# A graph layer whose second half is moved into the turns of its gathers

## The reference

```python
xn = layernorm(x)
def gnn_layer(x, row, col, W, b, g, beta):
    agg = segment_sum(x[col], row)              # one gathered row per edge
    deg = maximum(segment_sum(1, row), 1)
    h = (x + agg / deg) @ W.T + b
    return silu(layernorm(h) * g + beta)
x = x + gnn_layer(gnn_layer(xn)) + mix(xn)      # mix: per-node QKV, small blocks, w_res, hyperbolic scalings
y = layernorm(x)
w = softmax(((y @ W_x + b_x) @ W_slice + b_slice) / temp)   # 8 heads x 64 slices per node
token = normalised sum over nodes of w * (y @ W_fx + b_fx)
out_slice = attention(token)                    # 8 small 64x64 attentions
x = x + (sum over slices of w * out_slice) @ W_out + b_out
```

## Time and profile before

| | |
|---|---|
| median of 3 runs | 2936.33 us (2932.64 to 2941.06) |
| profiled execution | 2949.13 us, span 2947.2 us |
| busy: PE, ACT, DVE, POOL | 75%, 55%, 48%, 56% of the span |
| mean granted TensorE clock | 0.873 |
| first gather of layer 0 | 298.3 us |
| last gather of layer 1 | 2423.3 us |

### The profile page before, as it was taken

The page is one execution under the profiler, slowest core; times in us unless marked ns, Lnnn a source line. Parts: engine busy times, 40 slices in busy tenths (PEclk is TensorE's granted clock), DMA queues, the critical chain, the costliest instruction groups (busy, mean ns, idle before and its releaser), DMA issues.

```text
span 2947.2 us, 34117 instructions
## 1 busy us (share of the span) xinstructions
PE 2224.6 (75%) x8923; PEld 1618.1 (55%) x8923; DVE 1404.6 (48%) x3188; ACT 1624.0 (55%) x3910; POOL 1645.6 (56%) x1745
## 2 busy tenths in 40 slices
PE   0776677777778787669487778778787658899999
PEld 0542456565656665555355656566565545455577
DVE  8899513443434443327523434344343215899611
ACT  7410465666666666536556666666666533565422
POOL 0000777777777777740477777777777771344300
PEclk9887688998888898878788989888898876899999
DMA  7200333333333333351333333333333347200002
GB/s 181 70 18 0 98 109 109 114 109 112 113 113 110 114 111 108 111 145 46 114 109 109 113 112 111 111 113 114 111 110 110 109 113 174 72 18 9 1 18 70
DMA packets 101271, 280.80 MB, mean 95 GB/s; under 512 B 29211, under 2 KB 43369, under 8 KB 97088
## 3 DMA queue, kind: packets, MB, share of 16 engines
q0 software_dynamic: 75904, 210.74, 25.1%
q1 hardware_dynamic: 12184, 55.08, 7.0%
q10 hardware_dynamic: 13000, 12.80, 1.5%
HBM read 252.91 MB, written 25.60 MB: 95 GB/s over the span
## 4 chain that ended last, share of the span: by engine, by line
POOL 50%; PE 17%; issue 17%; DVE 14%; DMA 1%; ACT 1%; DVEq 0%; ACTq 0%; SPq 0%; POOLq 0%
POOL big L566 50%; PE ps L1161 3%; PE ps L1262 3%; DVE arena_a L1296 3%; DVE arena_a L1297 3%; PE ps L1128 2%; PE ps L1150 2%; PE ps L1042 1%; PE ps L1144 1%; PE ps L1254 1%; PE ps L1159 1%; DVE big L1733 1%; DMA big<-table,arena_a 1%; DVE big L1734 1%; DVE lnst L1340 1%
## 5 line engine op out<-in xcount | busy, mean ns | idle before, releaser
L566 POOL DMA_INDIRECT big<-table,arena_a x1568 | 1509.6, 963 | 709.1 <-issue 476.7
L1042 PE MATMUL ps<-big 128*125 x3968 | 1073.5, 431 | 504.0 <-SPq L461 308.0
L1042 PEld LDWEIGHTS ps<-big 128*125 128x125 f32 x3968 | 833.3, 214 | 716.7 <-issue 565.4
L1629 DVE TENSOR_TENSOR big<-ps,big 125x257 f32 x496 | 211.0, 425 | 1263.5 <-PE ps L1042 1240.4
L697 ACT ACTIVATE arena_b<-iota_row,arena_a 128x125 f32<-128x125 f32 x1984 | 601.3, 386 | 62.2 <-PE ps L1042 28.2
L699 ACT ACTIVATE big<-arena_b,ones 128x1000 f32<-128x1000 f32 x248 | 280.0, 1129 | 8.1
L720 ACT ACTIVATE nodes<-nodes 125x512 f32<-125x512 f32 x50 | 31.6, 632 | 305.1 <-DVE nodes L1687 305.1
L1683 DVE RECIPROCAL nodes<-nodes 125x512 f32<-125x512 f32 x50 | 167.7, 3353 | 1.7
L1061 PE MATMUL ps<-arena_b,nodes 128*125 128x384 f32 x400 | 165.4, 538 | 0.0
L594 POOL TENSOR_TENSOR arena_b<-arena_b,head 125x512 f32<-125x512 f32 x50 | 55.0, 1100 | 161.9 <-DVE head L1741 161.9
L555 POOL IOTA big<- 1x992 f32 x1 | 0.9, 948 | 195.0 <-DVEq L1419 195.0
(11 more groups left out here) (387 smaller groups left out, 3159.7 us busy)
## 6 DMA issues: line engine op xcount, KB each, us to landing
big<-table,arena_a POOLq DMA_INDIRECT x1568
table<-nodes SPq DMA_DIRECT2D x9, 1120.0 KB
nodes<-table SPq DMA_DIRECT2D x4, 1680.0 KB
nodes<-table ACTq DMA_DIRECT2D x50, 125.0 KB
mix_rows<-nodes ACTq DMA_DIRECT2D x50, 125.0 KB
nodes<-in_x_dram SPq DMA_DIRECT2D x5, 1120.0 KB
big<-mix_rows SPq DMA_DIRECT2D x5, 1120.0 KB
nodes<-in_x_dram SPq DMA_DIRECT2D x10, 560.0 KB
```

The source lines that it names most:

```text
L566: pool.indirect_dma_start(gat[:, GRP * slot + k, 0:D], None, table[l], bass.IndirectOffsetOnAxis(ap=s_dst[:, n:n + 1], axis=0)).then_inc(s ...
L1042: mm = pe.matmul(ps[0:PT, SUM_BANKS[q % SB], 0:257], onehot[:, ROUND * (r % 2) + QS * k + n, :], gat[:, bass.ds(slots[QS * k + n], 1), :]. ...
L1629: dve.tensor_tensor(at, ps[0:PT, SUM_BANKS[q % SB], 0:257].unsqueeze(1), at, ALU.add).then_inc(s("agg_added"), 1)
```

## The change

- Tiles are ranked by their number of edges at the start: ScalarE counts for tiles 1 to 33, VectorE for the others; 50 rounds of "equal to t, times rank" on VectorE, added up by TensorE, give each edge its tile's rank, and the sort (levels 1 to 7 now behind this) goes by rank. `acc` of layer 1 is in order of rank; `order_row` turns a rank back into a tile number for transfers.
- Tile k's quads are complete by quad 5(k + 1).
- All 50 mix tiles stand in layer 0's window, one slot behind every half round (2 quads).
- In layer 1's window a planner (`second_layer_plan`) lists for 272 ticks, 248 of them with a quad, which of 16 stages of which tiles stand behind the quad on each engine: U (u), T (transpose), H (product), B (statistics), S and R (root and reciprocal for a group of tiles), Z (norm and Tanh), X (x2), V and Q (its root and reciprocal), C (normalised row), D (transpose), L (logits), M (maximum, subtraction, Exp), N (sum, reciprocal, product), W (sum over nodes). Quads of layer 1 use 2 banks instead of 4.
- The folds of the slice weights stand behind quads 0 to 3 of layer 1 (`set_up`).
- ScalarE starts the loads of x1, x and mix rows a few tiles ahead and stores x2 tile by tile; GpSimd does nothing in layer 1 but gather; the products that GpSimd made go to VectorE. x2 is read back at the end, and each output tile is stored by itself.

```diff
-SUM_BANKS = (3, 4, 5, 7)
+SUM_BANKS = ((3, 4, 5, 7), (6, 7))
+QUADS_A_TILE = 5
-NM = NT // 2
-EARLY = (0, 3)
+NM = NT
+HALVES = 2 * NSL // ROUND
+AHEAD = 2
...
+GROUPS = [6, 6, 6, 6, 6, 6, 5, 4, 2, 1, 1, 1]
+STAGES = ("W", "N", "M", "L", "D", "C", "Q", "V", "X", "Z", "R", "S", "B", "H", "T", "U")
+PE_COST = {"W": 1.9, "L": 1.0, "D": 0.35, "H": 1.4, "T": 0.35}
+DVE_COST = {"N": 1.6, "M": 1.5, "X": 1.8, "Z": 1.1, "S": 1.5, "V": 1.5, "B": 0.45, "U": 0.6}
...
+                if any(at.get(one, tick) >= tick for one in need):
+                    break
+                if st == "U" and tick < min(QUADS_A_TILE * (k + 1), NQ) - 1:
+                    break
+                if items and (pe + PE_COST.get(st, 0) > 2.3 or dve + DVE_COST.get(st, 0) > 3.1):
+                    break
...
+def window(step, slot):
+    for half in range(max(HALVES, SLOTS)):
+        if half < HALVES:
+            step(half)
+        if half < SLOTS:
+            slot(half)
...
-            for t in range(1, NT + 1):
+            for t in range(1, SUMMED):
                 ins = act.activation(counted, bin_f, ACT.Relu, bias=bin_id[0:PT, t:t + 1], scale=-1.0, accum_out=counts[0:PT, t:t + 1])
...
+            for t in range(NT):
+                pe.wait_ge(s("eq_made"), t + 1)
+                for k in range(2):
+                    mm = pe.matmul(ps[0:PT, k, 0:EQ // 2], ident_b[:, :], eq_ring[t % EQ_RING][:, k * EQ // 2:(k + 1) * EQ // 2], start=(t == 0), stop=(t == NT - 1))
+                mm.then_inc(s("eq_used"), 1)
...
+                    for tick, items in enumerate(PLAN):
+                        if tick % 2 == 0 and tick // 2 + AHEAD < NSG:
+                            onehots(tick // 2 + AHEAD)
+                        set_up(tick)
+                        for st, k in items:
+                            second_step(st, k)
+                        for st, k in PLAN[tick - 1] if tick else []:
+                            move_rows(st, k)
...
+                    if st == "L":
+                        pe.wait_ge(s("bank5_read"), BANK_READS["D", k])
+                        if k >= 1:
+                            pe.wait_ge(s("shifted"), k)
+                        pe.matmul(ps[0:PT, 4, :], ones3[:, 0:PT], lbias3[:, :], start=True, stop=False)
+                        for n in range(2):
+                            mm = pe.matmul(ps[0:PT, 4, :], xlT_ring[:, n, :], wc[:, n, :], start=False, stop=(n == 1))
+                        mm.then_inc(s("logits_made"), 1)
...
+                for t in range(NT):
+                    if t >= EQ_RING:
+                        dve.wait_ge(s("eq_used"), t - EQ_RING + 1)
+                    dve.tensor_scalar(eq_ring[t % EQ_RING], bin_b, float(t), rank[0:PT, t:t + 1], ALU.is_equal, ALU.mult).then_inc(s("eq_made"), 1)
...
+                    if st == "M":
+                        dve.wait_ge(s("logits_made"), k + 1)
+                        link(dve.tensor_reduce(head8[:, k % 2, 0, :], heads(ps[0:PT, 4, :]), AX.X, ALU.max))
+                        dve.wait_ge(s(f"x2_stored{k % 2}"), 16 * (k // 2 + 1))
+                        dve.tensor_tensor(each, logits, per_head(0).unsqueeze(3).to_broadcast([PT, 2, H // 2, G]), ALU.subtract).then_inc(s("shifted"), 1)
+                    if st == "N":
+                        dve.wait_ge(s("exp_done"), k + 1)
+                        link(dve.tensor_reduce(per_head(1), each, AX.X, ALU.add))
+                        link(dve.reciprocal(head8[:, k % 2, 2, :], head8[:, k % 2, 1, :]))
+                        dve.tensor_tensor(each, each, per_head(2).unsqueeze(3).to_broadcast([PT, 2, H // 2, G]), ALU.mult).then_inc(s("w_ready"), 1)
...
+            for k in range(NT):
+                tile = tile_of(k)
+                sp.wait_ge(s("out_ready"), k + 1)
+                for p in PARTS:
+                    sp.dma_start(out_d[p, tile, :], x2_all[p, k, :].unsqueeze(1)).then_inc(s("out_stored"), 16)
```

More of the change, by code:

```diff
@@ L133, in at_slot, with parity_count, slots_of @@
     return t if not odd and 0 <= t < NM else None
[L136 to L152, removed]
+def parity_count(t):
+    return t // 2 + 1
+def window(step, slot):
[4 more added lines that the diff above has]
+            slot(half)
 def tile_at(i, lag):
     return i - lag if 0 <= i - lag < NT else None
-def slots_of(l):
-    return NT + (LN_X + 4 if l == 1 else LN_Z + 1)
+def slots_of():
+    return NT + LN_Z + 1
 def group_due(i, lag):
@@ L414, in run_halves, with tile_numbers, tile_of @@
             return g[:, :, 0:gap], g[:, :, gap:2 * gap]
+        def tile_numbers(engine):
+            held = {}
+            def tile_of(k):
+                part = k // 16
+                if part not in held:
+                    held.clear()
+                    _, held[part] = nc.values_load_multi_w_load_instructions(
+                        order_row[0:1, part * 16:min(part * 16 + 16, NT)], [engine], min_val=0, max_val=NT - 1,
+                        skip_runtime_bounds_check_because="a tile's number, a sum of one-hot products")
+                return bass.ds(held[part][k % 16], 1)
+            return tile_of
         block = ctx.enter_context(nc.Block())
@@ L1000, in _ @@
                     half = NSL // 2
-                    for k in range(2):
-                        pe.matmul(ps[0:1, 4 + k, 0:half], ones[0:NT, 0:1], tcmp[:, k * half:(k + 1) * half], start=True, stop=True)
+                    each_quad = tcmp.rearrange("p (q c) -> p q c", c=QS)[:, :, 0]
+                    for k, step in enumerate((tile_step[:, :], ones[0:NT, 0:1])):
+                        pe.matmul(ps[0:1, 4 + k, 0:NQ], step, each_quad, start=True, stop=True)
                     for k in range(2):
@@ new lines, in _ @@
+                if l == 0:
+                    window(additions, mix_slot)
+                    dve.wait_ge(s("agg_added"), NQ)
+                    link(dve.tensor_scalar(cols[:, 3, :], acc[:, :, D], 1.0, None, ALU.max))
+                    link(dve.reciprocal(rdeg[:, :], cols[:, 3, :]))
+                    for i in range(slots_of()):
+                        post_slot(i)
+                    dve.wait_ge(s("silu_done"), NT)
+                else:
+                    factor_rows()
+                    for tick, items in enumerate(PLAN):
+                        if tick < NQ:
+                            addition(tick)
+                        set_up(tick)
+                        for st, k in items:
+                            second_step(st, k, tick)
```

951 lines of the change are left out of this document (563 added, 388 removed).

## The result

The changed kernel takes 3020.1 us (median of 4 runs, 3015.9 to 3024.3) beside 2938.7 us of the kernel before (2932.6 to 2941.4): ratio 1.028, interval 1.0254 to 1.0306. It is slower by 81 us; the forecast was faster by 62, and its range ended at 2995.

What follows compares the result with a forecast made beforehand. The prediction took GpSimd's successive gathers to bound both windows, and 360 us of later work to move under them. Its terms: 54 + 90 + 90 - 300 + 4 = -62, from 2936 to 2874 us; range 2775 to 2995.

Steps and rivals of the forecast that it cites:

- part 2: Layer 0's window: a loop of waits through o takes 18.5 us a tile against the gathers' 16.0; +90 us, range +40 to +170.
- the ring's four groups: Layer 0's window: the gather ring holds 32 gathers, 40 us; with the last 23 half rounds, GpSimd's lead saves about 60.
- Setup: Before the first gather: the sort of levels 1 to 7 now waits for ranking and counts; +54 us, range +37 to +76.
- Between the layers: Between the two gather windows: same code, the folds covered by light early quads; 0 us, or 20 without that cover.
- Layer 1: Layer 1's window: logits and softmax wait for each other in dense ticks; +90 us, range +10 to +180.
- the tick of 7.6 us: Layer 1's window: a tick with L, M and N takes 7.6 us, not the 4.0 that gathers need.
- X ticks and bank 5: Layer 1's window: ticks with three additions, a bn_stats and row loads, plus turns of bank 5, add about another 100 us.
- Tail: After layer 1's last quad: the 360 us shrink to 60, range 50 to 80; -300 us.
- Output: Last matmuls and stores: x2 reads hidden, smaller last store -2, TensorE's lower clock +6; +4 us.
- The gathers hide everything: Both windows: rival in which loop and ticks stay within 16.0 and 4.0 us; 2694 us, chance 0.12.
- The gathers slow down: Mainly layer 1: rival in which VectorE operations with two SBUF operands lengthen gathers; +25 on top, 2899 us, chance 0.09.
- The dense ticks set the whole window: Layer 1's window: rival in which neither GpSimd's lead nor light ticks help; +265 instead of +90, 3049 us, chance 0.19.

Runs made afterwards that it cites:

- the kernel with the loop cut: Changed kernel with ScalarE's square of o moved behind the copies of rT and s in layer 0's window: 2820.9 us, ratio 0.9597.
- the run with 28 transposes: Changed kernel with 28 needless transposes on TensorE ahead of its wait for rT in layer 0's window: 2945.3 us, ratio 1.000.

## Why the prediction was wrong

**The step that failed is part 2, layer 0's window, +90 us.** The mechanism was right: the loop through o, on the engines and lines named, binds 47 times. Its size was not.

- *The turn.* Predicted 18.5 at full clock and 0.7 for the clock, 19.2; measured 20.6. The prediction counted ScalarE up to the second copy of rT and put 0.2 behind it, a term that no row shows. In the changed kernel that copy ends at 1011.93 and the QKV product starts 0.9 us later, at 1012.83. Between them stands the copy of s, for which the code makes the same product wait. It stands behind the copies of rT in the kernel before too, there hidden beside TensorE's quads, which end at 908.62:

```profile
901.41 7.21 PE L1042 MATMUL ps<-big 128*125 x32 [0.34 <-SPq L461]
...
907.64 0.82 ACT L732 ACTIVATE nodes<-ps 125x768 f32<-125x768 f32 x1
```

The copy is worth 0.6 us a turn.

- *The clock.* The mean of the window (0.86) was spread over TensorE's work, 0.7 us. But the clock falls behind the loop's own wait, so the slow products all stand on the loop. It is 1.6 us instead of 0.7, as the run with 28 transposes shows.
- *What is given back.* The prediction took off 60 us for the ring's four groups and the last half rounds. 47 turns x 4.6 = 216 us. Against the kernel with the loop cut (1020.2) the window is 203 longer, so 13 came back. The traces say why: at the QKV product of the last tile GpSimd had started 656 gathers, and 643 in the kernel with the loop cut. It was 13 gathers (16 us) further, not the ring's 32. Another 10 us (1020.2 against 1010.5) are in neither sum and stay unexplained. 66 (47 x 1.4) + 47 + 10 make up the 122.

**The prediction gave 21 us a tile as the end of its range** and took the middle of a loop without slack. That end, +170, would still have been short, for the 60 us that it also takes off. One of its signs was wrong too: it expected ScalarE's wait for o to be "gone small", but a loop that runs through o keeps that wait. It is 5.0 us a tile (251.4 over 50), before 6.1.

The other steps:

- *Setup*, +42 for +54. A ranking round costs 0.36 us on VectorE (50 between 59.2 and 77.2), not 0.6. One instruction (L1528, 800 elements of bf16) takes 422 ns and overlaps with the next. Of the three bounds, 0.3, 0.58 and 0.99, the one for bf16 was the nearest.
- *Between the layers* 0, and the folds covered: right. That they would cost 20 us without the cover was not: 3019.7 us with the folds first.
- *Layer 1*, +103 for +90: right in size and mechanism. Inside it the shares were off: the addition behind the quad costs 77 and N and the rest 19 to 37, where the tick of 7.6 us had 2.3 and 1.6 us. The items "X ticks and bank 5" (about 100) and what was set against them (60 and 35) are not needed: with M first nothing of the loss is left. That they all but cancelled was luck.
- *Tail*, 73.9 us for 60: inside its range of 50 to 80; where the other 14 us went is not known. The Trainium skill, "ScalarE: Activation LUTs", section "What ACT_TABLE_LOAD costs", states a drain of about 1.38 us for each switch. By the prediction's estimate from it the tail would be 71 us, nearer to the 73.9, but the trace doesn't show the drain:

```profile
2826.33 1.28 ACT L953 ACT_TABLE_LOAD   x1
2827.63 0.29 ACT L953 ACTIVATE cols<-cols 125x1 f32<-125x1 f32 x2
2827.94 1.28 ACT L972 ACT_TABLE_LOAD   x1
2829.23 0.63 ACT L972 ACTIVATE whole<-whole 125x512 f32<-125x512 f32 x1
```

Two loads and their activations follow each other with at most 0.02 us between, so a switch costs 1.3 us here.

- *Output*, +2 for +4: right. TensorE is busy 145.4 us there instead of 139.3, at a clock of 0.94 instead of 0.98, which is the +6 of the prediction.

- *Rivals.* The gathers hide everything: false for the changed kernel, but with two edits of queue order its 2694 us was reached within 17. The gathers slow down: false, over layer 1's 784 gathers their mean is 956 ns, before 961. The dense ticks set the whole window: false, its window would be about 1,273 us, not 1,111. That rival's total, 3049, lies nearer to 3020 than the forecast's 2874, but only by chance: the loss is in the other window. It was the forecast's own mechanism, larger.

## What to carry to other kernels

When work is packed closer so that a loop of waits between engines becomes the limit, add up every instruction that stands between the loop's wait and its release on each queue, then look for the instruction in the loop that could stand behind the release: here one square and one maximum, moved past a few others, were worth 304 of 3015 us. A wait that repeats in such a loop can be paid twice on TensorE, once as idle time and once in the lower clock behind it; take the second price from rows that stand behind such a wait (here 1.6 us a turn), not from the window's mean (0.7). And measure a tuned order on more than one chip.

## What the hardware did that was not expected

- TensorE's granted clock fell to 0.5 behind waits of 3.5 us in all 47 turns of the changed kernel, behind waits of about 2.9 us in 33 of 47, and behind waits of about 1.8 us that followed 1.9 us of small transposes in 42 of 45. With all but 0.5 us of the wait filled by transposes it stayed at 1.00 in all 45, and 3.15 us of needless work a turn made the kernel some 70 us faster (3015 to 2945, on two chips; ratio 1.025 to 1.000).
- Between chips: the same kernel before took 2937 to 2946 us in four comparisons and 3227 and 3232 in two, and the ratio of the same two kernels was 0.922 on one chip and 1.015 and 1.017 on two others.
